# First attention block: tiles 10 to 31 of x read as 32x32 squares, normalised in that order and transposed by VectorE in place of TensorE; two activation buffers of the second block change roles

## What is computed

```python
h = _sln(hidden, w, ...)            # (h - mean) / sqrt(var + eps), then gamma(w) * . + beta(w)
qkv = (h @ Wqkv.T + bqkv)           # q, k, v: 16 heads of 32
energy = jnp.einsum('bhqd,bhkd->bhqk', q, k)
att = jax.nn.softmax(energy, axis=-1) / D ** 0.5
out = jnp.einsum('bhqk,bhkd->bhqd', att, v)
h1 = out @ Wp.T + bp + hidden
return _sln(h1, w, ...) + h1
```

```python
h = film(rmsnorm(x, norm1_w), cond, film1_w, film1_b)
x = x + softmax(Q @ K.T * D ** -0.5) @ V @ proj_w + proj_b
h = film(rmsnorm(x, norm2_w), cond, film2_w, film2_b)
return x + gelu(h @ mlp_w1 + mlp_b1) @ mlp_w2 + mlp_b2
```

## Time and profile before

| what | us |
|---|---|
| median of 3 runs | 1479.72 |
| lowest and highest run | 1478.57, 1479.89 |
| the profiled execution | 1478.36 |
| its span, first to last instruction | 1476.5 |

### The profile page before, as it was taken

How to read it: one execution, slowest core, us unless ns; L and a number is a source line. 1 busy time by engine, 2 the same in 40 slices (tenths; PEclk the granted TensorE clock), 3 DMA queues, 4 the chain that set the end, 5 groups by cost and what they waited for, 6 DMA issues and landing times.

```text
span 1476.5 us, 24231 instructions
## 1 busy us (share of the span) xinstructions
PE 1467.3 (99%) x8714; PEld 1194.1 (81%) x8714; DVE 935.3 (63%) x1878; ACT 669.8 (45%) x2024; POOL 621.9 (42%) x544
## 2 busy tenths in 40 slices
PE   8999999999999999999999999999999999999999
PEld 5888888888888668888888788888888888888887
DVE  6677777777776676887767644763458434763354
ACT  4656556555553454656665433332324323332210
POOL 5756666766654556766846102401123102401001
PEclk9999999999999999999999999999999999999999
DMA  7222232232213534797544855545454545545342
GB/s 259 69 76 98 72 105 75 80 101 73 76 69 122 199 144 131 258 326 262 189 170 151 313 206 192 158 157 214 164 193 141 193 186 179 163 159 216 132 137 92
DMA packets 92792, 232.58 MB, mean 158 GB/s; under 512 B 9664, under 2 KB 17856, under 8 KB 87552
## 3 DMA queue, kind: packets, MB, share of 16 engines
q1 hardware_dynamic: 90848, 216.24, 42.5%
q10 hardware_dynamic: 1824, 14.79, 2.4%
HBM read 174.17 MB, written 56.82 MB: 156 GB/s over the span
## 4 chain that ended last, share of the span: by engine, by line
PE 97%; DVE 1%; POOL 1%; issue 0%; ACT 0%; POOLq 0%
PE bank L728 20%; PE bank L730 20%; PE bank L729 20%; PE bank L1234 7%; PE bank L1238 7%; PE bank L1236 7%; PE bank L819 4%; PE bank L812 2%; PE bank L830 2%; PE bank L1156 2%; PE bank L1051 1%; PE bank L869 1%; PE bank L861 1%; PE bank L743 1%; PE bank L1187 1%; POOL xa L2296 1%
## 5 line engine op out<-in xcount | busy, mean ns | idle before, releaser
L1343 ACT ACTIVATE pa<-bank,neg_max 128x128 f32<-128x128 f32 x512 | 181.2, 407 | 133.7 <-DVE neg_max L1753 133.7
L728 PE MATMUL bank<-w_hi,g_hi 128*128 128x512 f32 x512 | 200.6, 392 | 0.0
L730 PE MATMUL bank<-w_hi,g_lo 128*128 128x512 f32 x512 | 199.4, 390 | 0.0
L729 PE MATMUL bank<-w_lo,g_hi 128*128 128x512 f32 x512 | 199.4, 390 | 0.0
L1234 PE MATMUL bank<-op_hi,ring 128*128 128x512 f32 x448 | 174.9, 390 | 0.6 <-DVE op_lo L1658 0.3
L1238 PE MATMUL bank<-op_hi,ring 128*128 128x512 f32 x448 | 174.5, 390 | 0.0
L1236 PE MATMUL bank<-op_lo,ring 128*128 128x512 f32 x448 | 174.5, 389 | 0.0
L2341 POOL TENSOR_TENSOR pa<-pa,rec 128x512 f32<-128x512 f32 x128 | 142.9, 1125 | 52.3 <-DVE rec L1776 52.2
L2313 POOL TENSOR_TENSOR xrc<-xrc,b 128x512 f32<-128x512 f32 x32 | 49.7, 1585 | 269.1 <-DMA xrc<-x_dram 269.1
L1606 ACT ACTIVATE sum<-sum,cols 128x512 f32<-128x512 f32 x128 | 92.0, 722 | 114.0 <-DVE sum L2179 113.9
L1343 ACT ACTIVATION_READ_ACCUMULATOR pa<-bank,neg_max 128x1 f32 x512 | 126.5, 247 | 0.0
(11 more groups left out here) (266 smaller groups left out, 3541.0 us busy)
## 6 DMA issues: line engine op xcount, KB each, us to landing
ring<-w_dram SPq DMA_DIRECT2D x32, 1792.0 KB, 7.5
rows<-st_dram SPq DMA_DIRECT2D x32, 512.0 KB, 4.2
hid_dram<-sum SPq DMA_DIRECT2D x64, 256.0 KB, 2.2
hid<-hid_dram SPq DMA_DIRECT2D x64, 256.0 KB, 2.7
w_dram<-w_parts ACTq DMA_DIRECT2D x8, 1792.0 KB, 6.1
xa<-xt_in SPq DMA_DIRECT2D x32, 256.0 KB, 4.1
xra<-xt_in SPq DMA_DIRECT2D x32, 256.0 KB, 2.8
x_dram<-h SPq DMA_DIRECT2D x32, 256.0 KB, 2.0
```

The costliest lines, as they stand in the source:

```text
L728: nc.tensor.matmul(dst, w_hi, a_hi, start=start, stop=False)
L729: nc.tensor.matmul(dst, w_hi, a_lo, start=False, stop=False)
L730: return nc.tensor.matmul(dst, w_lo, a_hi, start=False, stop=stop)
L1343: last = nc.scalar.activation(pa[:, j, m, :], scores_bank[j][:, m * P:(m + 1) * P], ACT.Exp, bias=neg_max[:, j * C + m:j * C + m + 1], acc ...
```

## The change

1. `TURN` = 10. For tiles n = 10 to 31 the four TensorE transposes (`norm_a` on TensorE) are gone. The tile is loaded a second time by `load_squares`: four DMAs of 32 partitions each, in runs of 32 floats (128 bytes), so that each 32x32 square lies where it belongs in the transposed tile, itself not yet transposed. GpSimd normalises it there with four operations over 128x(4x32) (`norm_squares`), and VectorE's `turn` transposes within the squares, 128x512 from `xa` to `hf`. ScalarE's `scale_a` then reads and writes `hf` in place.
2. Since tokens now lie across partitions and squares, mean and reciprocal deviation must be spread: `stats_a` on GpSimd writes them to `stat_rows` (the power and two operations on 128x4), TensorE's `spread_stats` is one f32 matmul with the 128x128 weights `same_lane` and 8 columns, and VectorE's `copy_stats` takes the 8 columns from PSUM. The plain load for the statistics stays (`load_stat`), with its statistics one step earlier (tile t + 10 in step t).
3. `xa` is used as two tiles for squares and two for statistics. `load_squares` waits for `x_turned`: the tile two before it has been turned.
4. `make_squares` builds the two constants, three VectorE operations ahead of the loop.
5. In the second block `hb_new` and `hb` become `hb[0]` and `hb[1]`, which change roles from group to group; the copy at L1512 and both waits for `hb_copied` are gone.

```diff
+            def load_squares(n):
+                if n < TURN + 2:
+                    sp.wait_ge(n_done, n - 1)
+                else:
+                    sp.wait_ge(x_turned, n - TURN - 1)
+                src = tokens(xt, n).rearrange("(w j) (c q i) -> q j c w i", j=SQ, c=C, i=SQ)
+                for q in range(P // SQ):
+                    sp.dma_start(xa[q * SQ:(q + 1) * SQ, n % 2].rearrange("j (c w i) -> j c w i", c=C, i=SQ), src[q])\
+                        .then_inc(x_in[n % 2], 16)
...
-                if t + 3 * GB - 1 < NB:
-                    load_x(t + 3 * GB - 1)
+                if t + TURN < NB:
+                    load_squares(t + TURN)
+                if t + TURN + 1 < NB:
+                    load_stat(t + TURN + 1)
...
+            def spread_stats(n):
+                pe.wait_ge(rstd_ready, n + 1)
...
+                nc.tensor.matmul(x_bank[:, 0:2 * P // SQ], same_lane[:], stat_rows[:, n % 2], start=True, stop=True)\
+                    .then_inc(n_done, 1)
...
-                if t + AHEAD < NB:
+                if t + AHEAD < TURN:
...
                 attend(t)
+                if t > 0 and t + AHEAD + 1 < NB:
+                    spread_stats(t + AHEAD + 1)
...
+            def turn(n):
+                dve.wait_ge(xn_ready, n + 1)
+                dve.wait_ge(lo_ready, n - 1)
+                nc.vector.transpose(h_full(n).rearrange("p c t -> p (c t)"), xa[:, n % 2]).then_inc(x_turned, 1)
...
+                if TURN <= t + AHEAD < NB:
+                    turn(t + AHEAD)
                 if t > 1:
                     add_x1(t - 2)
                 if t > 0:
                     residual(t - 1)
+                if t > 0 and t + AHEAD + 1 < NB:
+                    copy_stats(t + AHEAD + 1)
...
+            def norm_squares(n):
+                i, w = n % 2, P // SQ
+                pool.wait_ge(n_scaled_dve, n - TURN + 3)
+                pool.wait_ge(x_in[i], squares_in(n))
+                tile = xa[:, i].rearrange("p (c w i) -> p c w i", c=C, i=SQ)
+                for k in range(w):
+                    last = nc.gpsimd.tensor_scalar(tile[:, :, k], tile[:, :, k], stat_lanes[:, i, k:k + 1],
+                                                   stat_lanes[:, i, w + k:w + k + 1], ALU.subtract, ALU.mult)
...
             for t in range(NB):
+                if TURN <= t + AHEAD < NB:
+                    norm_squares(t + AHEAD)
                 if t < NB - 1:
                     add_bias(t, t % 2, xra, bp0, xr_in[t % 2], loaded(t // 2 + 1), xr_ready)
...
-                if t + AHEAD + 1 < NB:
-                    norm_a(t + AHEAD + 1)
+                if t == 0:
+                    norm_a(TURN - 1)
+                if t + TURN < NB:
+                    stats_a(t + TURN)
...
-                nc.scalar.activation(hb[:], hb_new[:], ACT.Identity).then_inc(hb_copied, 1)
```

More of the change, by code:

```diff
@@ L379, in block_pair_kernel @@
         hid_out, HID_OUT = stage_in, 32
-        hid_in, HID_IN = x_in, 16 * NG
+        hid_in = x_in
+        HID_IN = [16 * loads_a(i) for i in range(GB)]
         y_out, Y_OUT = x1_out, 16 * NG
@@ L476, in _ @@
             sp.wait_ge(st_stored, 16)
-            for n in range(2 * GB, 3 * GB - 1):
+            for n in range(2 * GB, TURN):
                 load_x(n)
+            load_stat(TURN)
             sp.wait_ge(wa_lo_made, 5)
@@ L1155, in body_b @@
                     for k in range(C):
-                        last = nc.tensor.matmul(ps_s[b % 2][:, 0:P], tb[:, k, tok], hb[:, k, tok], start=(k == 0),
+                        last = nc.tensor.matmul(ps_s[b % 2][:, 0:P], tb[:, k, tok], hb[g % 2][:, k, tok], start=(k == 0),
                                                 stop=(k == C - 1 and not first))
@@ L1870, in film_table @@
                 nc.vector.memset(tmp_b[:, 0, 0:1], 0.0).then_inc(st_made, 1)
+            make_squares()
             for t in range(NB):
@@ L2286, in scales, with then, stats_a @@
                     .then_inc(cur, 1)
+            pool_steps = [0]
+            def then(instruction):
+                pool_steps[0] += 1
+                instruction.then_inc(pool_step, 1)
+                pool.wait_ge(pool_step, pool_steps[0])
+            def stats_a(n):
+                i = n % 2
+                pool.wait_ge(var_ready, 2 * n + 2)
+                then(nc.gpsimd.tensor_tensor(rstd1[:, i:i + 1], ve1[:, i:i + 1], neg_half[:, 0:1], ALU.pow))
+                if n >= TURN + 2:
+                    pool.wait_ge(n_done, n - 1)
+                w = P // SQ
+                nc.gpsimd.tensor_scalar(stat_rows[:, i, 0:w], in_square[:], mv1[:, i, 0:1], None, ALU.mult)
+                nc.gpsimd.tensor_scalar(stat_rows[:, i, w:2 * w], in_square[:], rstd1[:, i:i + 1], None, ALU.mult)\
+                    .then_inc(rstd_ready, 1)
+            def norm_squares(n):
[6 more added lines that the diff above has]
+                                                   stat_lanes[:, i, w + k:w + k + 1], ALU.subtract, ALU.mult)
+                last.then_inc(xn_ready, 1)
             def norm_a(n):
@@ L2410, in rest_first @@
                 pool.wait_ge(rq_made, NB - GB)
[L2411 removed]
+                then(combine(t1, h_late[:, 0:2, own], hb[0][:, 0:2, own]))
                 then(combine(t2, h_late[:, 2:C, own], t1))
[L2413 removed]
+                combine(n4, hb[0][:, 2:C, own], t2).then_inc(t_made, 1)
             def body_b(g, first, last):
```

115 lines of the change are left out of this document (74 added, 41 removed).

## The result

The change makes the kernel slower. Its median is 1507.1 us (four runs, 1504.3 to 1509.0) against 1479.2 us for the kernel before: a ratio of 1.0187, with a 95% interval of 1.0169 to 1.0205. I had forecast 1474.7 us, with a range up to 1484.0. So the direction was wrong, and so was the range. The profiled execution has a span of 1504.7 us, 28.2 us above the one before.

What follows compares the result with a forecast made beforehand. It took TensorE's own instructions as the bound (97% of the span). With -6.2 us on TensorE, 0.3 at the start and 0.9 for late `xra` landings, about -5.0 us, it forecast 1474.7 us, range 1471.6 to 1484.

Steps and rivals of the forecast that it cites:

- TensorE's share: First block: dropping four transposes saves 0.48 us a step, the spread matmul costs 0.20; net 0.28, 6.2 us over 22 steps.
- T: Length of a first-block step, from scores to scores: forecast 15.22 us, against 15.50 before.
- rival 4: The spread matmul on TensorE costs 0.35 us, so a step takes 15.37 and the kernel 1476.8 us; chance 0.12.
- VectorE: Transpose of 128x512 takes 0.70 us a step (upper end 1.2), plus a small copy; the next row maxima are not late.
- From the turn to the `xra` issue: SyncE's queue: four square loads 2.12 us, statistics' load and store 0.47 each, so `xra` is issued at 16.93.
- The landing: The `xra` tile lands 2.76 us after its issue plus 0.2 of queueing, at 19.89 us from the step's start.
- An overrun of x costs x/2 a step: TensorE's wait at the last softmax part: lateness beyond the margin is paid only by half, as it also lengthens the step.
- margin of 0.22: Last softmax transposes: the scales end at 25.76 us, TensorE wants them at 25.98; before, the margin was 0.55 us.
- GpSimd: Four normalising pieces take at least 2.08 us, covered before the `xra` tile lands; `add_bias` takes 1.29, the scales 4.58.
- ScalarE, the second block, the start: ScalarE covered by 1.2 us; second block's dropped copy worth nothing (0 to -0.7 us); start costs 0.3 us (0 to 1).
- rival 1: The load queue becomes the bound through late `xra` loads: path 1.5 us longer, step 15.86, kernel 1487.6 us; chance 0.18.
- Rival 3: Short packets of the square loads move slowly, so the `xra` tile lands 1.2 us later than before: 1484.3 us; chance 0.08.

Runs made afterwards that it cites:

- squares_behind_xra: The changed kernel with each tile's square loads issued one step later, behind the `xra` load: 1474.0 us, ratio 0.9956 to 0.9981 to the kernel before.
- runs_of_2kb: The changed kernel with the four square loads in the same place but in runs of 2 KB, not 128 bytes (output meaningless): 1490.7 us.
- issues_added: The changed kernel with two tiny loads (128 runs of 16 bytes each) added ahead of the `xra` load in steps 1 to 22: 1522.0 us.
- roles_only: The kernel before with only the second block's two buffers changing roles and no copy: 1478.8 us, ratio 0.9990 to 1.0007.
- held_load_on_before: The kernel before with its x tile load split into four issues that wait for the same step's residual, ahead of the next `xra` load: 1497.3 us.

## Why the prediction was wrong, step by step

- **TensorE's share**: right. The transposes' 0.48 us a step is gained: wherever nothing waits, a step without spread matmul takes 15.00 to 15.03 us. The matmul costs 0.32 us, not 0.20, but inside my bounds of 0.11 and 0.35. T would have been 15.34 by my sum, and the undisturbed step is 15.32. That is rival 4; by my sum it would have given 1476.8, and squares_behind_xra, where nothing else is late, measured 1474.0.
- **VectorE**: right. The turn takes 0.70 us, 22 times out of 22, and the copy of the statistics 0.17. The Trainium skill, "VectorE: DVE Perf Modes", section "The three transpose paths", has a figure for 128x128 in bf16, from which I had estimated 1.24 us; the trace has 0.70 for 128x512 in f32, and the measurement decides.
- **From the turn to the `xra` issue**: wrong, 3.06 us forecast and 4.26 in the mean of 20 steps. I priced the square loads by four loads of w1 in 512 runs of 512 bytes (2.12 us). They take 2.7 to 3.9 (2.7 in most steps), and the statistics' load behind them 0.66 or more (up to 1.6) rather than 0.47. Why loads with as many runs differ here I can't say; the row was the nearest, and it was taken without a bound above it.
- **The landing**: wrong, 2.96 us forecast and 4.16 measured (issue to `add_bias`, 3.5 to 5.6). I took the median of loads that had no other load close ahead of them, only a store (in step 18 issued 1.4 us earlier, at 324.69), and 0.2 for the queue. Now 0.5 MB (squares and statistics) are issued in the 3.8 us ahead of it (333.29 to 337.08), and a store too. runs_of_2kb has the same landing (4.24) with the same bytes in long runs, so the shortness of the runs isn't its main cause; the bytes queued ahead are what is left, and issues_added, which lets them drain longer, lands sooner (3.73). That is argued from these runs, not shown: none of them changes the bytes alone.
- **"An overrun of x costs x/2 a step"**: wrong; lateness on this path is paid in full, twice what I put. I kept the turn at 13.84 after the start of its step. But the turn stands behind the copies of the last softmax transposes, so when PE waits for those, the turn moves by the same wait, and nothing is given back in the next round. My own numbers already closed a ring. From the `scale_p` end at 25.76 through transposes, copies and the next turn at 13.84 + 15.22 = 29.06, less the margin of 0.22, is 3.08; with 3.09 for the issues, 2.96, 1.29 and 4.58 that is 15.00 us round, against PE's 15.22. The two terms above add 1.2 each, the others give 0.5 back: 15.00 + 1.20 + 1.20 - 0.52 = 16.88. A ring that is longer than PE's work sets the step, in full, as the table under issues_added bears out. With the two terms right and the rule of half kept, the step would have been 15.32 + (16.88 - 15.32) / 2 = 16.10: still slower than before, by 0.6 a step or some 13 us. So the two terms turned the sign, and the rule hid the other half of the loss, in the prices of rivals 1 to 3 too.
- **GpSimd**: right where it mattered. `add_bias` took 1.28 (1.29 forecast) and the scales 4.48 (4.58). The four normalising pieces took 3.42 us, 0.85 each, inside 2.1 to 4.2; they end 2.21 us ahead of the `xra` tile. In squares_behind_xra they are what `add_bias` follows; the last scale there still waits 0.67 us for VectorE's reciprocals, so they don't bind.
- **ScalarE, the second block, the start**: right. PE never waited for ScalarE in these steps, the copy was worth nothing (roles_only), and step 3 starts 0.44 us later than before although step 2 gained 0.18, which makes 0.6 us for the start (0.3 forecast, bounds 0 and 1).
- **The rivals**: rival 1 named the ring and where it would be seen, and I gave it 0.18 and 1487.6 us. With the full rule in place of the half its own 1.5 us would have made T 15.00 + 1.5 = 16.5, and 1479.7 + 22 x 1.0 = 1501.7. Rival 3 is refuted as put: the landing behind 2 KB runs is no shorter, and off the path short runs cost nothing. The Trainium skill's rule on transfers under 512 bytes, which I had cited there ("DMA: Bandwidth & Descriptors", section "Specifications"), doesn't show in the kernel's time. It does agree with the engines' busy share between 110 and 390 us, 0.39 against 0.34 at the same rate, though no run shows by what means. What short runs cost the kernel is 0.2 us of issue time per load. By that they do have a part in the loss, 16 of the 33 us that the order costs, as runs_of_2kb measures.
- **What stays open**: why the stretch of the issues varies between 3.6 and 5.0 us and the landing between 3.5 and 5.6 in a kernel whose steps do the same work, and by which rule the queue's issue time depends on runs and bytes.

## What to carry to other kernels

Before a queued instruction is given a new wait, follow what stands behind it until the path comes back to that wait. If it does, add up the ring and compare it with the bound engine's step; the larger is the step, and no half of an overrun is given back. A load that waits for this step's work belongs behind those that the next step needs first: that order alone turned +1.9% into -0.3% here.

## What the runs showed of the hardware

- The issue time of a load on SyncE's queue depended on its runs (medians): 421 ns for 32 runs of 2 KB, 637 ns for 512 runs of 128 bytes, and 435 ns for 128 runs of 16 bytes (the spare loads, median of 44).
- 128-byte runs, 42,240 of them more in a kernel, cost no device time where nobody waited for their issue (1474.0 against 1473.9 us), though the DMA engines were busier for the same bytes (0.39 against 0.34 of 110 to 390 us).
- Runs of 128 bytes that adjoin at both ends of the transfer were moved in longer packets, though the access was written in short ones (held_load_on_before: 1,009 packets more, not 40,320).
- A VectorE transpose within 32x32 squares of 128x512 f32 takes 0.70 us, the time of an addition of that size (0.69 to 0.71). An f32 matmul of 8 columns shows as two rows and costs 0.32 us between others; one of 16 columns in fp32r shows as one row and costs 0.23.
- TensorE's granted clock fell to 0.50 for a few us in step 3 of the change, after 4.5 us in which PE was busy for 2.4; other steps with waits at the same place kept 1.00.
